# Spectral mixing of a feature map on one core: TensorE's loop in rounds of five steps, ScalarE's branch and both ends moved, and the soft threshold in two rectified halves on ScalarE

## The reference

```python
# x: (4, 128, 128, 768) float32; 8 blocks of 96 channels
xf = jnp.fft.rfft2(x, axes=(1, 2), norm='ortho').reshape(b, h, wf, 8, 96)
xr, xi = jnp.real(xf), jnp.imag(xf)
o1r = relu(xr @ w1[0] - xi @ w1[1] + b1[0])
o1i = relu(xi @ w1[0] + xr @ w1[1] + b1[1])
o2r = o1r @ w2[0] - o1i @ w2[1] + b2[0]
o2i = o1i @ w2[0] + o1r @ w2[1] + b2[1]
# per block; then v -> v - lambd, v + lambd or 0, with lambd = 0.01
xc = softshrink(o2r, LAMBD) + 1j * softshrink(o2i, LAMBD)
return jnp.fft.irfft2(xc, s=(H, W), axes=(1, 2), norm='ortho') + x
```

## Time and profile before

| | |
|---|---|
| median of 3 runs | 4975.89 us (4975.51 to 4977.45) |
| the profiled execution's own time | 4975.77 us |
| its span | 4973.7 us |
| TensorE busy, weight loads busy | 4779.5 us (96%), 3997.2 us (80%) |
| VectorE busy | 4070.3 us (82%) |
| ScalarE busy | 2514.4 us (51%) |
| GpSimd busy | 1028.1 us (21%) |
| chain that ended last, by engine | PE 85%, DVE 6%, issue 5%, ACT 3%, POOL 1% |

### The profile page before, as it was taken

One profiled execution on the slowest core, in us unless ns is written; L12 is line 12 of the kernel. 1 busy time (PEld: TensorE's weight loads), 2 busy tenths in 40 slices (PEclk: granted clock), 3 DMA queues, 4 the chain that ended last, 5 costly groups with the idle time before them and its releaser, 6 DMA issues.

```text
span 4973.7 us, 120408 instructions
## 1 busy us (share of the span) xinstructions
PE 4779.5 (96%) x44930; PEld 3997.2 (80%) x44930; DVE 4070.3 (82%) x6763; ACT 2514.4 (51%) x4290; POOL 1028.1 (21%) x836
## 2 busy tenths in 40 slices
PE   6999999999999999999999999999999999999997
PEld 5888888888888887888878788788888888788886
DVE  5888888888888888888888888788887888888876
ACT  4554455545555445555445554455544555445553
POOL 0220222211222112222022220122211222102222
PEclk9999999999999999999999999999999999999999
DMA  6422544324443234442344423444224453234522
GB/s 110 102 60 51 107 104 104 77 45 95 103 103 87 43 86 103 103 99 44 74 103 103 108 50 62 101 103 108 63 61 88 103 108 78 59 76 103 107 53 51
DMA packets 1079029, 421.33 MB, mean 85 GB/s; under 512 B 1076128, under 2 KB 1076256, under 8 KB 1078432
## 3 DMA queue, kind: packets, MB, share of 16 engines
q1 hardware_dynamic: 1073696, 411.61, 39.1%
q10 hardware_dynamic: 4736, 1.60, 0.1%
HBM read 210.19 MB, written 201.33 MB: 83 GB/s over the span
## 4 chain that ended last, share of the span: by engine, by line
PE 85%; DVE 6%; issue 5%; ACT 3%; POOL 1%; SPq 0%; ACTq 0%; DMA 0%; DVEq 0%; POOLq 0%
PE ps L515 14%; PE ps L611 13%; PE ps L493 10%; PE ps L536 10%; PE ps L620 6%; PE ps L548 5%; PE ps L594 5%; PE ps L582 4%; PE ps L646 3%; PE ps L561 3%; PE ps L569 2%; PE ps L562 2%; ACT rings L733 2%; DVE ydg L954 1%; DVE biased L929 1%
## 5 line engine op out<-in xcount | busy, mean ns | idle before, releaser
L1051 POOL TENSOR_TENSOR whole<-whole 128x480 f32<-128x480 f32 (+1 forms) x416 | 499.4, 1200 | 3904.0 <-DVE whole L979 3904.0
L743 ACT COPY ydg<-ps 128x512 f32<-128x512 f32 (+4 forms) x1024 | 588.3, 578 | 571.4 <-PE ps L494 352.9
L611 PE MATMUL ps<-wts,hbig 128*128 128x192 f32 x4160 | 735.1, 328 | 4.3
L493 PEld LDWEIGHTS ps<-tab,rings 128*64 128x64 f32 x6144 | 675.3, 138 | 78.8 <-ACT rings L733 42.7
L493 PE MATMUL ps<-tab,rings 128*64 128x128 f32 x6144 | 701.2, 275 | 35.1 <-ACT rings L733 34.2
L515 PE MATMUL ps<-tab,rings 128*128 128x128 f32 x6144 | 712.1, 280 | 15.9 <-DVE rings L949 15.9
L515 PEld LDWEIGHTS ps<-tab,rings 128*128 128x128 f32 x6144 | 708.0, 196 | 18.8 <-DVE rings L949 17.9
L494 PE MATMUL ps<-tab,rings 128*63 128x128 f32 x6144 | 701.4, 275 | 0.0
L611 PEld LDWEIGHTS ps<-wts,hbig 128*128 128x128 f32 x4160 | 672.1, 190 | 20.6 <-ACT hbig L791 13.7
L494 PEld LDWEIGHTS ps<-tab,rings 128*63 128x63 f32 x6144 | 675.0, 137 | 0.0
L929 DVE TENSOR_TENSOR biased<-ps,wts 128x768 f32<-128x768 f32 (+1 forms) x544 | 498.9, 917 | 194.0 <-PE ps L620 189.4
(11 more groups left out here) (82 smaller groups left out, 8893.8 us busy)
## 6 DMA issues: line engine op xcount, KB each, us to landing
out<-whole SPq DMA_DIRECT2D x704, 240.0 KB, 4.2
whole<-in_x SPq DMA_DIRECT2D x384, 384.0 KB, 6.5
whole<-in_x SPq DMA_DIRECT2D x64, 408.0 KB, 7.8
whole<-in_x SPq DMA_DIRECT2D x64, 360.0 KB, 6.7
out<-whole SPq DMA_DIRECT2D x64, 216.0 KB, 3.5
wts<-in_mix SPq DMA_DIRECT2D x16, 513.0 KB, 4.9
out<-whole SPq DMA_DIRECT2D x64, 120.0 KB, 3.2
out<-whole SPq DMA_DIRECT2D x64, 96.0 KB, 2.9
```

The costliest lines, as they stand in the source:

```text
L493: pe.matmul(o[0:HALF], slot[:, 0:HALF], mat("fwd_w"), start=True, stop=True)
L611: mm = pe.matmul(o, hbig[:, k * H:(k + 1) * H], mix_part("w2_big"), start=first, stop=False, skip_group_check=True)
L743: act.copy(*line_moves(stage, g)).then_inc(line_act, 1)
L1051: pool.tensor_tensor(xs[p][:, a:b, :], u, xm, ALU.add).then_inc(y_plus, 1)
```

## The change

- TensorE's loop over 15 steps becomes 3 rounds of 5 steps written out (`UNROLL`).
- ScalarE no longer waits for the last inverse rows and issues row 0's transfers at the end of its step. It does so in the forward lines, ahead of group 6 (`MOVE_ROW0_AT`), so that its branch stands right behind the five ring packs.
- The waits on GpSimd's batches ahead of the mixing are spread: each stands ahead of the instruction that writes over the rows of that batch.
- `shrink` is cut in three: `add_bias`, the threshold, and `shrink`, which subtracts. For parts 1 to 15 (`NR`) ScalarE makes the threshold's two halves from v: relu(v - lambd) into `above`, then relu(-v - lambd) over v in place (`rectify`); VectorE subtracts the second from the first. Parts 16 and 17 keep VectorE's clamp. ScalarE's rectifying of group u stands in iteration u + 3, VectorE's subtraction of a group's first part at the end of iteration u + 2 and that of the second in iteration u + 3. `above` is one buffer, so a part's rectifying waits for the part before to be subtracted.
- The first x: SyncE issues the transfers of the even half, ScalarE those of the odd half, ahead of everything else in its queue.
- In the last unit GpSimd makes only 6 of the 13 groups of rows; VectorE makes the other 7 after its own halves (`last_sums`).

The diff, cut to its core:

```diff
 NP = len(PARTS)
+NR = NP - 2
...
+        above = over("above", [128, 8 * CB], F32, area, 60 * H + 16 * CB)
         edge = over("edge", [128, 2, 2 * CB], F32, area, 60 * H + 24 * CB)
...
-                    a, e = i * LOAD_ROWS, (i + 1) * LOAD_ROWS
-                    for lo, hi in ((a, e + (e == HALF)), (H + 1 - e, H + 1 - max(a, 1))):
-                        for t in range(2):
+                    for lo, hi in piece_rows(i):
+                        for t in parts:
                             sp.dma_start(xs[p][t * HALF:(t + 1) * HALF, lo:hi, :],
                                          src[t, :, lo:hi, :]).then_inc(x_loaded[p][i], 16)
...
 
-                load_x(0, 0, 0)
+                for i in range(PIECES):
+                    load_piece(0, 0, 0, i, (0,))
                 sp.dma_start(tab[:, FWD:TABLE], table[:, FWD:TABLE]).then_inc(table_loaded, 16)
...
                 to_inverse(0, 0, 0)
-                with pe.Fori(0, STEPS - 1) as t:
-                    step(t, False)
+                with pe.Fori(0, (STEPS - 1) // UNROLL) as rounds:
+                    for i in range(UNROLL):
+                        step(rounds * UNROLL + i, False)
                 step(STEPS - 1, True)
 
...
                     for g in range(NG):
+                        if stage == 0 and g == MOVE_ROW0_AT:
+                            move_row0(q)
                         if mover(stage, g) == "act":
                             act.wait_ge(line_done, lines_before(q, stage, g) + 1)
...
                 def move_row0(q):
+                    act.wait_ge(uv_ready, NF * q + NF)
...
                     act.dma_start(ydg[127:128, :, :], row0[:]).then_inc(row0_moved, 16)
                     act.dma_start(yedge[127:128, 0:4:2, :],
                                   row0[0:2]).then_inc(row0_moved, 16)
...
-                    if u == 0 and h == 0:
-                        wait_batch(act, q - 1, NF - 1)
...
                 def round_small(q, u):
+                    if u == 0:
+                        wait_batch(act, q - 1, 1)
                     act.wait_ge(zsmall_done, NU * q + u + 1)
                     if u >= 2:
                         act.wait_ge(big_mixed, NU * q + u - 1)
...
                     act.wait_ge(big_mixed, NU * q + u + 1)
-                    if u:
+                    if u == 0:
+                        wait_batch(act, q - 1, 7)
+                    else:
...
                                    bias=b1[0:r, 1:2]).then_inc(hsmall_ready, 1)
+
+                def rectify(q, u, h):
+
+                    at = part_at(u, h)
+                    n = halves(u) * len(part_pairs(u, h)) * 2 * CB
+                    act.wait_ge(bias_done, NP * q + at)
+                    if at > 1:
+                        act.wait_ge(shrunk, NP * q + at - 1)
+                    v = biased[at % 2][:, 0:n]
+                    act.activation(above[:, 0:n], v, ACT.Relu, bias=threshold[:])
+                    act.activation(v, v, ACT.Relu, bias=threshold[:],
+                                   scale=-1.0).then_inc(rectified, 1)
 
                 def step(t, last):
...
                             if it < NU:
-                                for h in range(2):
-                                    if (it, h) in PARTS:
-                                        copy_big(q, it, h)
+                                copy_big(q, it, 0)
+                            if 3 <= it:
+                                rectify(q, it - 3, 0)
+                            if it < NU:
+                                if (it, 1) in PARTS:
+                                    copy_big(q, it, 1)
                                 round_big(q, it)
+                            if 3 <= it and (it - 3, 1) in PARTS:
+                                rectify(q, it - 3, 1)
+                            if it < NU:
                                 round_small(q, it)
                             if it >= 1:
...
+                first = x[0:1, :, :, 0:CB].rearrange("o h (m t) c -> (o t) m h c", t=2)
+                for i in range(PIECES):
+                    for lo, hi in piece_rows(i):
+                        act.dma_start(xs[0][HALF:W, lo:hi, :], first[1, :, lo:hi, :]).then_inc(x_loaded[0][i], 16)
                 act.wait_ge(cleared, 1)
                 act.wait_ge(pairs_folded, FOLDS)
                 for g in range(RING):
                     pack_lines(0, 0, g)
                 copy_row0(0)
-                move_row0(0)
                 with act.Fori(0, STEPS - 1) as t:
                     step(t, False)
...
                     dve.wait_ge(zsmall_hi_ready, NU * q + u + 1)
+                    if u == 0:
+                        wait_batch(dve, q - 1, 4)
                     dve.tensor_tensor(zsmall_lo[u % 2][0:r, 0:n], ps[0:r, z_bank(u, "small"), 0:n],
...
+
+                    return pairs, ne, m, at, parts
+
+                def add_bias(q, u, h):
+                    _, ne, m, at, parts = part_views(u, h)
                     d = ps[:, out_banks(u, h), 0:ne * 2 * CB][:, 0:m].rearrange("p i (k c) -> p i k c", c=2 * CB)
                     b2 = mix_part("b2").rearrange("p (i k c) -> p i k c", i=1, k=1).broadcast_to([128, m, ne, 2 * CB])
                     dve.wait_ge(mix2_done, NP * q + at)
-                    if at > 1:
-                        dve.wait_ge(shrunk, NP * q + at - 1)
+                    if at > 2:
+                        dve.wait_ge(shrunk, NP * q + at - 2)
+                        if at - 2 <= NR:
+                            dve.wait_ge(rectified, NR * q + at - 2)
                     else:
                         wait_batch(dve, q - 1, NF - 1)
-                    dve.tensor_tensor(parts(v), d, b2, ALU.add).then_inc(bias_done, 1)
+                    dve.tensor_tensor(parts(biased[at % 2]), d, b2, ALU.add).then_inc(bias_done, 1)
+
+                def clamp(q, u, h):
+                    _, ne, m, at, _ = part_views(u, h)
+                    n = m * ne * 2 * CB
                     dve.wait_ge(bias_done, NP * q + at)
-                    dve.tensor_scalar(c, v, LAMBD, -LAMBD, ALU.min, ALU.max).then_inc(clamp_done, 1)
-                    dve.wait_ge(clamp_done, NP * q + at)
+                    dve.tensor_scalar(above[:, 0:n], biased[at % 2][:, 0:n], LAMBD, -LAMBD,
+                                      ALU.min, ALU.max).then_inc(clamp_done, 1)
+
+                def shrink(q, u, h):
+                    pairs, ne, m, at, parts = part_views(u, h)
+                    if at <= NR:
+                        dve.wait_ge(rectified, NR * q + at)
+                        plus, minus = parts(above), parts(biased[at % 2])
+                    else:
+                        dve.wait_ge(clamp_done, (NP - NR) * q + at - NR)
+                        plus, minus = parts(biased[at % 2]), parts(above)
                     first = 0
                     if (u, h) == (EDGES, 0):
-                        e = parts(c)[:, :, 0, :]
-                        dve.tensor_tensor(e, parts(v)[:, :, 0, :], e, ALU.subtract).then_inc(edge_ready, 1)
+                        e = minus[:, :, 0, :]
+                        dve.tensor_tensor(e, plus[:, :, 0, :], e, ALU.subtract).then_inc(edge_ready, 1)
                         dve.wait_ge(edge_ready, q + 1)
                         halves_of = edge[:].rearrange("p k (r c) -> p k r c", r=2)
...
 
+                def last_sums(q, p, g):
+                    a, b = odd_rows(g)
+                    u, xm = ucopy[g][:, 0:b - a, :], mirror(xs[p], a, b)
+                    dve.wait_ge(uv_ready, NF * q + NF + g + 1)
+                    dve.tensor_tensor(xs[p][:, a:b, :], u, xm, ALU.add).then_inc(last_plus, 1)
+                    dve.wait_ge(last_plus, g - POOL_LAST + 1)
+                    dve.tensor_tensor(xm, u, xm, ALU.subtract).then_inc(batch_ready[batch_of(g)], batch_part(g))
+
                 def wait_loaded(p, times, i):
...
+                                shrink(q, it - 3, 1)
+                            add_bias(q, it - 2, 0)
+                            if (it - 2, 1) in PARTS:
+                                add_bias(q, it - 2, 1)
                             if it in FOLD_IN and fold_next:
                                 fold_in(q, t, p, it)
+                            shrink(q, it - 2, 0)
+                        for u in range(NU - 2, NU):
+                            add_bias(q, u, 0)
+                            clamp(q, u, 0)
+                            shrink(q, u, 0)
                         dve.wait_ge(shrunk, NP * q + NP)
                         lines(q, p, 1)
                         for g in range(NF):
                             add_halves(q, p, g)
+                        if not fold_next:
+                            for g in range(POOL_LAST, NF):
+                                last_sums(q, p, g)
                         if fold_next:
                             to_mixing(q + 1, t + p, 1 - p)
 
...
 
-                with pool.Fori(0, STEPS) as t:
-                    step(t)
```

(43 more changed lines are left out.)

16 lines of the change are left out of this document (5 added, 11 removed).

## The result

The changed kernel takes **4996.0 us** (median of 6 runs, 4991.3 to 5004.5) against 4977.7 (6 runs, 4975.5 to 4979.1) of the kernel before on the same chip: ratio **1.0039**, 95% interval 1.0026 to 1.0052, slower by 0.4%. The forecast was 4990, slower. The profiled execution took 4999.5 with a span of 4997.4.

The account below looks back on a forecast made before the run. TensorE was taken to set the end almost everywhere, with loop branches costing 100.2 us. Terms: 4973.7 - 45 - 48 + 99 + 15 - 2 - 4 = 4988.7 span, forecast 4990 us, range 4936 to 5036 (own range 4968 to 5015).

Parts of the forecast that it names:

- TensorE's loop: At TensorE's loop branches: 14 backward branches become 2, saving 45 us, bounds 0 and -52.
- ScalarE's branch and row 0's transfers: Forward stages behind ScalarE's branch: all become 22.05 us, -48; row 0's transfers leave the first forward stage, -2.
- The ends: First image's loads from two queues: 0 (-6 to +3); last sums partly on VectorE: -4 (0 to -6).
- the engines are full, a second issuer adds nothing: First image's loads: DMA share 1.31 and 220 GB/s taken as full, so a second queue gains 0 (-6 to +3).
- The chain: Short groups ending the mixing: rectifying serial across ScalarE and VectorE, +3.1 us a unit, +99 us over 32 units.
- The clock: Half-clock stretches of TensorE behind two new gaps a unit, 1.85 and 2.2 us: +15 us, bounds 0 and +45.
- 64 gaps x 3/14: TensorE's new gaps: three of 14 earlier gaps drew a 1.1 us half-clock stretch, applied to 64 gaps: +15 us.
- In the steady groups ScalarE has room: Steady mixing groups: both rectifying pairs fit into ScalarE's idle time, and TensorE loses nothing there.
- Partly hidden: Rival, end of mixing: hand-overs partly hidden by VectorE ready early, no clock loss; 4943 us, chance 0.19.
- ScalarE the bound in every group: Rival, mixing groups: a pair over 2.3 us pushes each second ScalarE copy, +80, 5070 us; chance 0.09.
- no unrolling gain: Rival, TensorE's loop: the stall returns in straight code, +45, 5035 us; chance 0.09.
- Costs nothing: Rival, mixing: TensorE's queue covers the rectifying and the 0.92 us wait goes; 4848 us, chance 0.08.

Follow-up runs that it names:

- The kernel without rectifying: Changed kernel with VectorE clamping all 17 parts in the order of before, all else of the change kept: 4857.5 us, ratio 0.9762.
- fifteen steps in a row: Changed kernel with VectorE clamping every part and 15 steps unrolled in TensorE's loop in place of 5: 4851.8 us, ratio 0.9751.
- the rectifying alone: Changed kernel with loops, row 0's transfers and both ends put back as before; rectifying on ScalarE and split waits for GpSimd's batches left: 5059.3 us, ratio 1.0171.
- TensorE kept busy: Changed kernel with 13 in place of 4 matmuls with no user ahead of the inverse lines: 4977.3 us, ratio 1.0004.
- the kernel with the second pair moved: Changed kernel with ScalarE's copy of group 8 ahead of part 14's pair of rectifyings in the mixing's last iteration: 5059.6 us, ratio 1.0169.

## Why the prediction was right, point by point

The time and the sign were right, and the mechanism was the one named. But two groups of terms were too small, one by 19 us and one by 25, with opposite signs. That 4990 lies 6 us from the measurement is in part luck. (The sum itself gives 4990.9.) The kernel without rectifying shows both.

*What the rest saves.* The sum had -45 - 48 - 2 - 4 = -99. Measured together: 4857.5 - 4975.2 = -117.7.
- TensorE's loop: -45 forecast, -41.7 alone. "Nothing in mid-body shows a fetch stall, so straight code is costed at nothing" held: fifteen steps in a row brought no stall of TensorE's own either.
- ScalarE's branch and row 0's transfers: -48 - 2 forecast, -51.6 alone; the first forward stage went from 25.30 to 23.61 us. The trace of after shows the cheaper case that was chosen: row 0's transfers are issued at 502.1 and 502.7 while the copies go on.
- The ends: 0 - 4 forecast, -9.3 alone. The step that failed is "the engines are full, a second issuer adds nothing": 0 (-6 to +3) was forecast for the first loads, and the first matmul moved by 8.5 us. A DMA share of 1.31 was read as a full resource, but with two queues the same engines moved 325 GB/s at 1.17. The Trainium skill, "DMA: Bandwidth & Descriptors", section Issuing engines are not separate DMA queues, says that issuing from several engines saves only the issuing time. On these loads the measurement differs as far as the trace can tell, and it decides: SyncE's issuing of the sixteen does fill 25.90 us before, but the first three issues take 0.66 to 0.89 us each and the later ones 1.67 to 1.98. The later ones seem to wait for room, and then issuing is not what set the rate. The tail gave 2.3 us, not 4 (from TensorE's last rows to the end of the span 25.7, before 28.0).
- Those three alone add up to -102.6. Another 15 us came only in the kernel that has all of them and the split waits for GpSimd's batches, which were costed at 0. About half of it lies in the mixing: from its first matmul to its last it takes 91.82 us against 92.03 before (medians), 7 us over 32 units. ScalarE's wait for GpSimd, 48.4 us in the earlier trace rows, is gone from it. That the split waits did it was not tried alone, and neither was the other thing that this kernel has and before has not: a part's bias waits for the subtract two parts back and not for that of the part before.

*What the rectifying costs.* Forecast 99 + 15 = 114; on top of the rest it is 4996.0 - 4857.5 = 138.5.
- The chain: 3.1 us a unit forecast. 152.88 against 149.49 are 3.4, 108 us; against the kernel before, on which the forecast stood, 2.86. The pieces came out as written: the pair 0.94 + 0.92 less the overlap (1.77 from start to end), the wait for the big copy 1.75 (1.85 forecast), the gap ahead of the lines 2.2 (2.2).
- The clock: +15 forecast against 38.3 - 17.8 = +20 relative to before, and 35 against the kernel without rectifying. The step "64 gaps x 3/14" took all gaps alike. In fact 20 of the 30 gaps of 2.2 us drew a stretch, and one of the 32 of 1.75 us. This share was not a constant of the gap either: with the rectifying alone four of 15 gaps of 2.2 us drew one, and four of 32 of 1.75 us.
- "In the steady groups ScalarE has room" is shown: parts 1 to 10 cost 1.5 us in all. All but that lies in parts 11 to 15.

*What the sum left out.* It added parts that are not independent. Alone, unrolling gives 41.7 and rectifying costs 84.1. But TensorE's stall at its branch stands just where it waits for the ring copy, in 14 units. With the late ring copy of the changed kernel, unrolling takes away 74.2 - 70.1 = 4 us of waiting; without it, (39.0 + 15.9) - (5.6 + 25.3) = 24. That is 20 us. The clock behaves alike. TensorE's busy time in the inverse lines, from the pages of before, the rectifying alone, the kernel without it, and after:

```profile
L515 PE MATMUL ps<-tab,rings 128*128 128x128 f32 x6144 | 712.1, 280 | 15.9 <-DVE rings L949 15.9
L527 PE MATMUL ps<-tab,rings 128*128 128x128 f32 x6144 | 712.7, 280 | 34.0 <-DVE rings L1001 34.0
L528 PE MATMUL ps<-tab,rings 128*128 128x128 f32 x6144 | 697.9, 277 | 22.1 <-DVE rings L1005 22.1
L528 PE MATMUL ps<-tab,rings 128*128 128x128 f32 x6144 | 732.7, 284 | 64.1 <-DVE rings L1005 64.1
```

Where the branches already drew the slow stretches, rectifying added 0.6 us to these lines; where the branches were gone, it added 34.8. The four single results (the split waits are in that of the rectifying) add up to 4975.2 - 41.7 - 51.6 - 9.3 + 84.1 = 4956.7, and the kernel takes 4996.0. The -45 and the +99 were both taken from units in which the other was absent. The forecast's +99, charged to all 32 units, was close for the unrolled kernel (108).

*The rivals.* "Partly hidden" (decides under 2.8 us a unit) came near, since 2.86 was measured; the clock tipped it. With TensorE kept busy the same chain gives 4977.3, no change. "ScalarE the bound in every group" is out by the parts 1 to 10, and "no unrolling gain" by the unrolling alone. "Costs nothing" is out for the change as it is, and 4859.0 is what it looks like when the five late parts stay on VectorE (4848 forecast).

## What to carry to other kernels

Moving work from a busy engine to an idle one is free only where the other one has slack in the order of time: put the split where the groups are long, and end it before the last groups, whose hand-overs are one serial chain (here ten parts were free and five cost 137 us). Free is not a gain: with ten parts moved the kernel took 4859.0 us and with none 4857.5, since TensorE had not been waiting for VectorE there. Two waits at one place do not add: before a stall is taken out, look at what is late behind it. And a gap of TensorE has two prices, the gap and the clock behind it; where the gap can't go, matmuls with no user in it gave back 17 to 19 us here.

## What the runs showed of the hardware

- Two issuing queues moved the first image's strided loads at 325 GB/s with a DMA share of 1.17. One queue, SyncE's or ScalarE's, moved 220 at 1.31.
- After gaps of 1.0 to 1.2 us (29 units of the kernel with parts 1 to 14 on ScalarE) TensorE's clock fell in none. After gaps of 2.2 us it fell in 20 of 30 units of the changed kernel, for 3.4 or 6.8 us at 1.2 GHz, but in 4 of 15 of the kernel with the rectifying alone. After the 1.75 us gaps it fell in 1, 2, 4 and 10 of 32 units of four kernels, most often in the one with 13 matmuls in the later gap. No run here explains the differences. After gaps of 0.5 to 2.9 us close together (the kernel with the second pair moved) it fell in every unit, in 21 of 32 for 10.2 us.
- A taken backward branch of TensorE's long loop took 3.3 to 3.7 us at the median and 4.0 at most in the kernels that had one; straight code of fifteen steps showed no such stall.
- ScalarE's relu of 128x768, SBUF to SBUF with the bias from a pointer, took 936 ns, and the next began 0.1 us before it ended. By the formula of the Trainium skill's "ScalarE: Activation LUTs" (section What ACT_TABLE_LOAD costs) it is an estimate of 920 ns, within 2% of this trace.
